# The second attention of a four-stage layer stack: unmasked keys, recall inside A x V, a split output projection, and eight last tiles that share the engines with the next layer

## The reference, cut to what matters

```
sq, sk = elu(q) + 1, elu(k) + 1                       # q, k, v = x @ w.T by heads
out_m = einsum('bhsd,mhde->mbhse', sq, memories)      # four memories
rel   = einsum('bhsd,mhd->mbhs', sq, memory_norms)
out_m = out_m / clip(rel, EPS, None)[..., None]
weights = softmax(rel.mean(axis=-1), axis=0)          # over a whole sequence
mem_out = einsum('mbhse,mbh->bhse', out_m, weights)
kv_cum, k_cum = cumsum(sk * v), cumsum(sk)            # linear attention, causal
local = einsum(sq, kv_cum) / clip(einsum(sq, k_cum), EPS, None)
out = g * mem_out + (1 - g) * local                   # g = sigmoid(gate)
x = x + out @ w_o.T
...
x = x + 0.5 * (gelu(x @ ternary(W1).T + b1) @ ternary(W2).T + b2)
```

## Time and profile before

| what | value |
|---|---|
| median of three runs | 2562.16 us (2555.75 to 2564.55) |
| profiled execution, its own time | 2559.23 us |
| its span | 2557.4 us |
| TensorE matmuls (PE) busy | 2432.3 us, 95% |
| weight loads (PEld) | 2130.6 us, 83% |
| VectorE (DVE) | 1862.6 us, 73% |
| ScalarE (ACT) | 1420.1 us, 56% |
| GpSimd (POOL) | 1284.5 us, 50% |
| mean granted TensorE clock | 0.985 |

### The profile page before, as it was taken

How to read it: one execution, slowest core, us unless ns; L and a number is a source line. 1 busy time by engine, 2 the same in 40 slices (tenths; PEclk the granted TensorE clock), 3 DMA queues, 4 the chain that set the end, 5 groups by cost and what they waited for, 6 DMA issues and landing times.

```text
span 2557.4 us, 78277 instructions
## 1 busy us (share of the span) xinstructions
PE 2432.3 (95%) x32360; PEld 2130.6 (83%) x32360; DVE 1862.6 (73%) x4374; ACT 1420.1 (56%) x2362; POOL 1284.5 (50%) x1398
## 2 busy tenths in 40 slices
PE   4999999999999979999999999989999999979999
PEld 3888888888888868888888999878888888858998
DVE  8999899677877789999985666545665566546664
ACT  4555555434333435556565888754444445418886
POOL 5878888621111148889986333213433443453331
PEclk9999999999999999999999999999999999979999
DMA  5000000010101110000000000000000000000111
GB/s 189 1 7 1 1 1 1 1 25 23 26 23 26 24 45 1 1 1 1 1 1 19 1 1 1 3 20 18 16 17 17 16 19 17 18 3 26 34 34 42
DMA packets 67728, 46.13 MB, mean 18 GB/s; under 512 B 13216, under 2 KB 66352, under 8 KB 67376
## 3 DMA queue, kind: packets, MB, share of 16 engines
q1 hardware_dynamic: 67376, 41.13, 5.8%
HBM read 15.91 MB, written 8.40 MB: 10 GB/s over the span
## 4 chain that ended last, share of the span: by engine, by line
PE 69%; issue 14%; POOL 11%; DVE 5%; ACT 2%; DMA 0%; POOLq 0%; SPq 0%; DVEq 0%; ACTq 0%
PE ps L46 12%; PE ps L48 12%; PE ps L47 12%; PE ps L1557 5%; PE ps L1555 5%; PE ps L1536 5%; PE ps L1535 4%; PE ps L618 3%; PE ps L270 3%; PE ps L1125 2%; POOL a1pry L2111 2%; POOL a1pry L2113 2%; POOL a1l L2099 2%; PE ps L1157 2%; POOL a1P L2107 2%
## 5 line engine op out<-in xcount | busy, mean ns | idle before, releaser
L1600 DVE TENSOR_TENSOR gHl<-gHf,gHh 128x512 fp32r<-128x512 f32 x256 | 187.1, 731 | 183.7 <-ACT gHh L1576 183.4
L237 POOL TENSOR_SCALAR ve<-mv 128x4 f32<-128x4 f32 x96 | 22.0, 229 | 573.0 <-DVE mv L227 568.8
L46 PE MATMUL ps<-WGH,XTH 128*128 128x512 f32 (+1 forms) x768 | 300.5, 391 | 7.4 <-ACT fSG L687 4.5
L48 PE MATMUL ps<-WGL,XTH 128*128 128x512 f32 (+1 forms) x768 | 290.9, 379 | 0.0
L47 PE MATMUL ps<-WGH,XTL 128*128 128x512 f32 (+1 forms) x768 | 290.0, 378 | 0.0
L687 ACT ACTIVATE fSG<-ps 128x704 f32<-128x704 f32 x128 | 97.0, 758 | 312.8 <-PE ps L48 312.8
L833 POOL TENSOR_TENSOR fHTL<-fHTF,fHTH 128x768 fp32r<-128x768 f32 x128 | 235.7, 1842 | 62.3 <-ACT fHTF L696 62.3
L1555 PE MATMUL ps<-W2T,gHh 128*128 128x256 f32 x1024 | 255.5, 283 | 0.0
L1557 PE MATMUL ps<-W2T,gHl 128*128 128x256 f32 x1024 | 253.0, 281 | 0.0
L2099 POOL TENSOR_TENSOR a1l<-a1l,a1rc 128x128 f32<-128x128 f32 x128 | 49.5, 407 | 361.2 <-DVE a1rc L2066 361.2
L46 PE MATMUL ps<-WDH,fHTH 128*128 128x256 f32 x768 | 221.8, 289 | 2.7 <-issue 2.7
(11 more groups left out here) (248 smaller groups left out, 7135.0 us busy)
## 6 DMA issues: line engine op xcount, KB each, us to landing
X<-in_x SPq DMA_DIRECT2D x16, 512.0 KB, 8.8
a0vp<-a0vt SPq DMA_DIRECT2D x256, 32.0 KB, 2.2
a1vp<-a1vk SPq DMA_DIRECT2D x256, 32.0 KB, 2.1
out<-X SPq DMA_DIRECT2D x16, 512.0 KB, 2.9
tws<-in_w SPq DMA_DIRECT2D x2, 1024.0 KB, 7.7
WN<-in_wgu SPq DMA_DIRECT2D x3, 384.0 KB, 6.7
a0km<-in_wqkv SPq DMA_DIRECT2D x2, 384.0 KB, 3.2
a1pry<-in_aw SPq DMA_DIRECT2D x1, 768.0 KB, 4.6
```

Source lines behind the costliest of these rows:

```text
L46: e.matmul(o, hh, mh, start=first, stop=False)
L48: return e.matmul(o, hh, ml, start=False, stop=last)
L1600: dve.tensor_tensor(Hl[m % 8][:, :], Hf[m % 4][:, :], Hh[m % 8][:, :].bitcast(F32), ALU.subtract).then_inc(s_hl, 1)
```

## The change

- **Unmasked keys.** TensorE transposes the two halves of the unmasked keys (`SK`, now two buffers) rather than four masked ones. `VK1` is 512 columns of keys and values and 32 ones. Growth contracts over the 64 tokens of its half; cross terms between heads are removed as the state leaves PSUM, by a product with the mask `own`.
- **Recall within A x V.** Recall stands between `values` and the denominators (`denominators`, split off). On DVE the `recalled` products move between the two state products, ahead of the masks.
- **Output projection by halves.** Y is transposed within `values_keys`, into the upper half of v's pair; ACT copies it to `YTH` as fp32r, DVE makes the low part `YTL`, and the projection is six fp32r matmuls with `OH` and `OL`. The order of the slots of the ring changes with it.
- **Beside.** From iteration 66 on the ring has two pairs; the third and banks 6 and 7 serve the first 11 units (`AHEAD`) of the layer S = 5, made between recall, Y transposes and output of iterations 66 to 73 (`beside`). Chunk 1 of that layer is normalized, turned and halved within the attention.
- **At the beginning of the attention** the first two projections stand within the last units of the layer S = 3.

The first loop over n below is TensorE's, the second DVE's.

```diff
+        beside = {66: (0, 1), 67: (2,), 68: (3, 4), 69: (5,), 70: (6, 7), 71: (8,), 72: (9,), 73: (10,)}
+        AHEAD = 11
         def slots1():
-            yield from [("p", 0, 0), ("p", 0, 1)]
+            yield from [("p", 0, 1), ("p", 0, 0)]
             for n in range(NT + FAR + 1):
                 i, j = n // 4 + 1, n % 4
+                far = [("m", n - FAR, 0), ("m", n - FAR, 1)] if 0 <= n - FAR < NT else []
+                if n > NT:
+                    yield from far
+                if n < NT or n > FAR:
+                    yield ("v", n)
+                if n == 0:
+                    yield ("t", i)
+                if n <= NT:
+                    yield from far
                 if n < NT:
-                    yield from [("v", n), ("s", n, 0), ("s", n, 1)]
-                far = [("m", n - FAR, 0), ("m", n - FAR, 1)] if 0 <= n - FAR < NT else []
-                yield from [("l", n), *far] if n < NT else [*far, ("l", n)]
...
+                    yield from [("s", n, 0), ("s", n, 1)]
+                if 0 <= n - 2 < NT:
+                    yield ("l", n)
...
+        two = ring1[("m", 66 - FAR, 0)]
+        in1 = lambda at: at % 3 if at < two else (at - two) % 2
...
         def emptied1(kind, n, g=0):
-            if kind == "l":
-                return ([(n_le, n - 1)] if 0 <= n - 2 < NT else []) + ([(n_yte, n - FAR)] if n > FAR else [])
+            if kind == "v":
+                return ([(n_vke, n + 1)] if n < NT else []) + ([(s_yl, NT + n - FAR)] if n > FAR else [])
...
             def values_keys(n):
...
-                if j == 0:
-                    pe.wait_ge(n_km, i + 1)
-                for h in range(2):
+                if n < NT:
                     for k in range(2):
-                        c = 256 + 256 * h + 128 * k
-                        ks = slice(256 * j + 128 * h, 256 * j + 128 * h + 128)
-                        t = pe.transpose(bank[:, c:c + 128], KM1[i % 2][:, k, ks], ident[:, :])
-                t.then_inc(n_vk, 1)
+                        mm3(pe, bank[:, 256:512], XTH[F % 2][:, k, ts], XTL[F % 2][:, k, ts],
+                            a1WH[:, k, 512:768], a1WL[:, k, 512:768], k == 0, k == 1)
+                    if j == 0:
+                        pe.wait_ge(n_el, 4 * i + 4)
+                    for k in range(2):
+                        t = pe.transpose(bank[:, 128 * k:128 * k + 128], SK[i % 2][:, k, ts], ident[:, :])
+                    t.then_inc(n_vk, 1)
+                if y >= 0:
+                    pe.wait_ge(n_p, 3 * y + 3)
+                    for k in range(2):
+                        t = pe.transpose(bank[:, 512 + 128 * k:640 + 128 * k], Y[y % 2][:, 128 * k:128 * k + 128],
+                                         ident[:, :])
+                    t.then_inc(n_yx, 1)
...
             def grow(m, h):
+                rows = slice(64 * h, 64 * h + 64)
                 for k in range(2):
                     for q in range(4):
-                        c = 256 + 256 * h + 128 * k + 32 * q
-                        t = pe.matmul(PS[7][32 * q:32 * q + 32, 36 * k:36 * k + 36], VK1[m % 2][:, c:c + 32],
-                                      VP1[m % 2][:, h, 4 * k + q:288:8], start=(j % 16 == 0 and k == 0), stop=True,
+                        c = 128 * k + 32 * q
+                        t = pe.matmul(PS[7][32 * q:32 * q + 32, 36 * k:36 * k + 36], VK1[m % 2][rows, c:c + 32],
+                                      VK1[m % 2][rows, 256 + 4 * k + q:544:8], start=(j % 16 == 0 and k == 0), stop=True,
                                       skip_group_check=True)
...
             for n in range(NT + FAR + 1):
+                if n > NT and r < NT:
+                    recall(r)
+                for u in beside.get(n, ())[:1]:
+                    ffn1_unit(pe, 5, u)
+                if n < NT or y >= 0:
                     values_keys(n)
+                for u in beside.get(n, ())[1:]:
+                    ffn1_unit(pe, 5, u)
...
                 if 0 <= m < NT:
                     grow(m, 0)
                     values(m)
+                if n <= NT and r >= 0:
+                    recall(r)
+                if 0 <= m < NT:
+                    denominators(m)
                     grow(m, 1)
                 if n < NT:
                     scores(n)
...
-                        t = pe.matmul(bank[:, 0:256], a1YT[y % 2][:, 128 * k:128 * k + 128], a1WO[:, k, :],
-                                      start=(k == 0), stop=(k == 1))
+                        ks = slice(128 * k, 128 * k + 128)
+                        t = mm3(pe, bank[:, 0:256], YTH[:, ks], YTL[:, ks], OH[:, k, :], OL[:, k, :], k == 0, k == 1)
...
             for n in range(NT + FAR + 1):
-                if 0 < n <= NT:
-                    state(2 * n - 2)
-                    state(2 * n - 1)
-                if n < NT:
-                    mask(n, 0)
-                    mask(n, 1)
...
+                if 0 < n <= NT:
+                    state(2 * n - 2)
+                if 0 <= r < NT:
                     dve.wait_ge(n_cf, r + 1)
                     recalled(r, 0)
                     recalled(r, 1)
+                if 0 < n <= NT:
+                    state(2 * n - 1)
+                for u in beside.get(n, ())[:1]:
+                    ffn1_unit_dve(dve, 5, u)
+                if y >= 0:
+                    dve.wait_ge(s_yh, NT + y + 1)
+                    dve.tensor_tensor(YTL[:, :], half1(1, "v", n)[:, 0:256], YTH[:, :].bitcast(F32),
+                                      ALU.subtract).then_inc(s_yl, 1)
+                for u in beside.get(n, ())[1:]:
+                    ffn1_unit_dve(dve, 5, u)
+                if n < NT:
+                    mask(n, 0)
+                    mask(n, 1)
...
-                    dve.tensor_copy(a1S[j % 4][:, :, 0:36],
-                                    PS[7][:, 0:72].rearrange("p (k v) -> p k v", k=2)).then_inc(n_ss, 1)
+                    dve.tensor_tensor(a1S[j % 3][:, :, 0:36], PS[7][:, 0:72].rearrange("p (k v) -> p k v", k=2),
+                                      own[:, :, :], ALU.mult).then_inc(n_ss, 1)
```

More of the change, by code:

```diff
@@ L164, in macaron @@
         sx = [sb(a1, f"a1sx{i}", [P, 16]) for i in range(3)]
-        S0 = sb(a1, "a1s0", [P, 2, 64])
-        a1S = [sb(a1, f"a1S{i}", [P, 2, 64]) for i in range(4)]
+        S0 = sb(a1, "a1s0", [P, 2, 32])
+        a1S = [sb(a1, f"a1S{i}", [P, 2, 64]) for i in range(3)]
         PRY = sb(a1, "a1pry", [P, 1536])
         RC = sb(a1, "a1rc", [P, 10, 80])
-        a1WO = sb(a1, "a1wo", [P, 2, D])
+        OH = sb(a1, "a1oh", [P, 2, D], R32)
+        own = sb(a1, "a1own", [P, 2, 36])
         MBC = sb(a1, "a1mb", [P, 2, 128])
@@ L1459, in attn1_set_dve @@
                 dve.wait_ge(s_on, 1)
+                dve.memset(own[:, :, :], 0.0)
                 for b in range(2):
@@ L1470, in attn1_set_dve @@
                 dve.wait_ge(s_mb, 1)
+                for k in range(2):
+                    for b in range(2):
+                        dve.tensor_copy(own[:, k, 16 * b:16 * b + 16], par[:, b:b + 1].broadcast_to([P, 16]))
+                        dve.tensor_copy(own[:, k, 32 + 2 * k + b:33 + 2 * k + b], par[:, b:b + 1])
                 for s in a1S:
-                    t = dve.tensor_copy(s[:, :, :], S0[:, :, :])
+                    t = dve.tensor_copy(s[:, :, 32:64], S0[:, :, :])
                 t.then_inc(s_mb, 1)
@@ L1522, in ffn1_unit @@
             i, f = m // 8, m % 8
-            if S == 5 and m == 0:
-                for s, v in emptied1(*order1[(len(order1) - 1) // 3 * 3]):
+            if S == 5 and m in (0, 11, 13):
+                for s, v in emptied1(*last1[{0: 2, 11: 1, 13: 0}[m]]):
                     pe.wait_ge(s, v)
@@ L1561, in ffn1_pe @@
         def ffn1_pe(pe, S):
-            for m in range(7 if S == 3 else 0, 8 * NS + LAG):
+            for m in range(7 if S == 3 else AHEAD, 8 * NS + LAG):
                 ffn1_unit(pe, S, m)
+                if S == 3 and m == 8 * NS - 1:
+                    attn1_ready(pe)
+                    attn1_proj(pe, 0, 0)
+                if S == 3 and m == 8 * NS + 1:
+                    pe.wait_ge(s_ge, 8 * NS)
+                    attn1_proj(pe, 0, 1)
         def ffn1_unit_act(act, S, m):
@@ L1585, in ffn1_unit_act @@
                 norm(act, *chunk(16 * S + i + 2), (f - 5,))
-            if S == 3 and f == 6 and 3 < i < 8:
+            if S == 3 and f == 6 and 3 < i < 9:
                 attn1_set_act(act, i - 4)
         def ffn1_act(act, S):
-            if S == 5:
-                act.wait_ge(n_mo, NT)
-            for m in range(5 if S == 3 else 0, 8 * NS):
+            for m in range(5 if S == 3 else AHEAD, 8 * NS):
                 ffn1_unit_act(act, S, m)
@@ L1618, in ffn1_unit_dve @@
                 v = i % 2
+                if S == 3 and i == NS - 1:
+                    attn1_elu(dve, 0, 0)
+                    attn1_elu(dve, 0, 1)
                 dve.wait_ge(s_d1, tb + q + 1)
@@ L1627, in ffn1_dve @@
         def ffn1_dve(dve, S):
```

(21 more changed lines are left out.)

256 lines of the change are left out of this document (139 added, 117 removed).

## The result

The change is slower. The changed kernel took a median of 2624.04 us (2619.63 to 2625.84, four runs) beside 2559.51 us for the kernel before on the same chip: a ratio of 1.0248, with a 95% interval of 1.0224 to 1.0273. The forecast was 2590 us and slower; the sign was right and the size too small by 34 us, outside the range.

What follows compares the result with a forecast made beforehand. TensorE's instruction order was taken to bound the second attention's middle. From 2559.2 us, +46 (middle: wait +61, saving -15), -9 (head) and -8 (tail) gave 2588, about 2590 with the median's offset; range 2532 to 2612.

Steps and rivals of the forecast that it cites:

- What bounds the kernel, and the sign: Second attention's middle: TensorE's instruction order sets it, others count only where TensorE stops for them; slower, chance 0.69.
- The wait at the scores: Middle tiles: scores wait for DVE's YTL to free their PSUM pair, 1.16 us a tile, +61 us.
- rival 3: Middle as forecast but waits lower the clock; five falls +17 us, 2607; chance with rival 2 together 0.09.
- What TensorE saves: Middle, 53 tiles: -0.53 saved, +0.24 for added shape changes, -0.29 us a tile, -15 us.
- key transposes and the wait for masked keys: Middle: two of four key transposes go, -0.22 us a tile; the wait for masked keys goes, -0.15.
- output projection and values after it: Middle: six fp32r products take the same 0.72 us; the value product after no longer starts late, -0.08 us a tile.
- growths, A x V, denominators: order and shapes: Middle: second growth no longer waits for the state copy, -0.08 us; two added shape changes, +0.24 us a tile.
- recall, enter, other transposes, turn, projections: Middle: recall, Y transposes and zero-state products called moved or hardly changed, nothing saved.
- rival 2: Array shape changes cost more than 0.13 us; +10 to +19 us, 2610 to 2617; chance with rival 3 together 0.09.
- Both faults in the middle: Middle's forecast sum: wait +61 and TensorE's saving -15, +46 us, 10.25 us a tile.
- The tail: Last attention tiles with units 0 to 10 merged in: 64.5 us against 72.9, -8 us (bounds -20, +3).
- The head: Tiles 0 to 10: earlier projections, shorter masked-key waits and a clock that stays up, -9 us (bounds -3 and -18).

Runs made afterwards that it cites:

- Experiment 1: Changed kernel with YTL earlier on DVE: ahead of both `recalled` products, 2557.4 us; between the two, 2551.07 us.
- experiment 2: Changed kernel with four useless products added on TensorE ahead of the scores in each tile from 11 to 63: 2582.94 us, ratio 1.0090.
- the kernel with YTL between: Changed kernel with DVE making YTL between the two `recalled` products, up to tile 65: 2551.07 us, ratio 0.9972.
- experiment 4: Changed kernel without feed-forward units beside the last tiles: 2622.05 us; the same with the ring kept at three pairs: 2605.22 us.
- experiments 5: Changed kernel with the units of the last tiles issued behind the tile's own chain on TensorE, ACT and DVE: 2607.88 us, ratio 1.0198.
- experiment 6: Changed kernel, YTL between `recalled` products: units behind the chain, 2542.71, again 2544.86 us; plus useless tail products, 2542.41; instead no units beside, three pairs, 2548.04.

## Why the prediction was right or wrong

The profiled execution took 64 us more than before where 29 were forecast. Of the 35 us between them 9.6 lie in the middle, 8 in the head, 13.9 in the tail and 3.4 in the rest of the last layer. The middle's 9.6 are small only because two larger faults in it have opposite signs.

- **What bounds the kernel, and the sign: right.** TensorE's order sets the middle, and the one wait that the ring of three brings makes the change slower. Experiment 1 shows it by removing it: moving YTL alone brings the time from 2624 to 2551.
- **The wait at the scores: right.** 1.16 us in 53 tiles were forecast, +61; measured 1.09, 57.9 us. Each link of the chain was within 0.14 us.
- **The clock (rival 3): the step that failed.** The prediction's sum kept the middle at full clock and so put this term at nothing; it gave rivals 2 and 3 together 0.09, and allowed the third five falls, +17. There were 20, and experiment 2 prices them at +31.4 us, which alone would have taken the forecast out of its range. The reasoning stopped at the size of one gap: a gap of 2.3 us had gone with a low clock, gaps of 0.5 had not, 1.1 lay between, so "some". It should have counted: a gap of 1.1 us in every tile is 53 occasions for a fall, and at 1.6 us a fall (31.4 / 20) even one in three is half the delay again.
- **What TensorE saves: mis-sized.** Forecast 0.29 us a tile, -15; measured 0.63, -32.7. By groups, distances from start to start added up over the 52 tiles and divided by them, before and in the kernel with YTL between (its wait of 0.40 taken off); both are at full clock throughout:

| part | forecast | measured |
|---|---|---|
| key transposes and the wait for masked keys | -0.37 | -0.49 (0.54 to 0.22; 0.69 in 12 tiles gone) |
| output projection and values after it | -0.08 | -0.16 |
| growths, A x V, denominators: order and shapes | -0.08 + 0.24 | +0.41 (1.63 to 2.05) |
| recall, enter, other transposes, turn, projections | 0 | -0.40 |

  The changes of shape cost nearly what was forecast where one can be read by itself: a first growth is followed by values after 0.38 us, 0.26 before, and values by the next group after 0.68, 0.52 before. So rival 2 fell. The second growth, for which -0.08 was forecast, starts 0.07 us later behind the denominators than before (0.57 for 0.50): the row that the forecast read had no wait in it. The last two rows belong together: recall takes changes of shape with it out of its old place and into the third row, and together they are +0.01 where +0.16 was forecast. "Nothing" for the last row was the fault: those groups were called moved or unchanged, and each takes 0.01 to 0.16 us a tile less in its new place, `enter` 0.16 and recall 0.11. Why each does was not tried.
- **Both faults in the middle:** +61 - 15 = +46 forecast; 56.9 - 32.7 + 31.4 = +55.6 measured. The saving too small and the clock left out nearly cancel, so the middle's sum looks better than its working.
- **The tail: wrong in sign.** -8 forecast, +5.9 measured. Tiles of 5.4 us, or 6.1 with two units, were forecast; they are 6.7 to 8.7 apart. The up products were priced at full clock and the down products, eight of 256 columns from unit 5 on, and the Y transposes behind them not at all. What stood in the change and was not asked: which pairs do recall and the Y transposes take with a ring of two? The output's and that of `recalled`, so recall waits for the addition to X and the Y transposes for `recalled` (experiment 4), together 1.36 us a tile. How much of the loss is the clock stays open (experiments 5 and 6).
- **The head: not settled by one pair of profiles.** -9 forecast, -1.0 at the start of tile 11. But that start lies between 1736.1 and 1746.4 us in eleven later profiles whose order up to there is the changed kernel's own or nearly so, 1742 on the mean with the changed kernel's 1746.3, against 1747.3 in the single profile of before: about -5. The two executions of one kernel in experiment 6 had 1744.9 and 1736.1. Most of that spread stands there before the attention begins: tile 0's key transposes start between 1646.9 and 1654.1 us in these twelve profiles (the changed kernel's with them), against 1654.1 before. From there to tile 11 it is 93.2 us before, and 93.5 in the changed kernel, 88.8 to 93.5 in the twelve, 91.1 on the mean. In the changed kernel the fall of the clock at 1719 us is gone, as forecast, but the one at the beginning lasts 13.7 us in place of 6.8.
- **Rest of the last layer:** +3.4 us, which no step had. In seven of the twelve profiles with the changed code it is 242.4 or 242.5 us, where before had 241.1; in the other five, the changed kernel among them, it is 244.1 to 244.7, and in just these the lower clock of the tail goes on for its first 3.3 to 4.7 us. So about 2 us are the clock, and the cause of the other 1.3 is open.

## What to carry to other kernels

When a transfer of a buffer makes the bounding engine wait a little in every tile, price three things: the wait, what the engine saves otherwise, and the clock: here 57 us of short waits cost another 31 us in clock. Then ask which instruction of the releasing engine is last and whether it can go between two longer ones: here one of 0.41 us, moved to stand some 0.7 us earlier, was worth 73 us. Where work is put beside a serial stretch, issue it behind the chain's own instruction on every engine, and count what giving up a buffer for it does to the chain. And when useless products are to fill a wait, look in the trace whether they stand ahead of the wait or behind it.

## What the runs showed of the hardware

- Waits of 1.09 us in each tile of some 10 us brought 20 falls of the clock of 3.4 us each in 52 tiles, and 17 to 20 falls with 58.0 to 68.3 us at the lower clock in the four kernels with the same waits. Waits of 0.40 us in each tile brought none in four profiles and one fall in a fifth; waits of 0.77 us in 25 tiles of 52 brought 10.2 us at the lower clock, waits of 1.28 us in 27 tiles (recall in its old place) 30.6 us; filled waits brought none.
- Filling TensorE's waits of the middle with products that nothing reads shortened that stretch by 31.4 us, although the wait was as long as before. In the tail added products raised the clock from 0.84 to 0.92 and nothing was gained; part of them stood behind the wait, in the chain.
- With a change of the array's shape between them a growth was followed by values after 0.38 us, without one after 0.26 (the growth's own shape differs too), and values by the next group after 0.68 us, without one after 0.52.
